# Two key projections moved in front of value products in a two-network attention kernel: the tensor engine's order changed, nothing else

## The reference, cut to what matters

```python
x = attn_layer(shift_tokens(x), Wqkv, q_scale, k_scale, Wo) + x
x = ffn_layer(shift_tokens(x), g, bln, W1, b1, W2, b2) + x

# attn_layer: 16 heads of 64, windows of 32 tokens
q, k, v = split(x @ Wqkv)              # 128 -> 3 * 1024
q = l2norm(q) * qs;  k = l2norm(k) * ksc
q = rotary(q);       k = rotary(k)     # with a scale per position
# each window of 32 queries sees its own and the previous 32 keys
sim  = where(mask, -big, q @ k.T * 8)
out  = softmax(sim) @ v
return out @ Wo
```

## Time and profile before

| what | value |
|---|---|
| median of 3 runs | 2304.53 us (2298.14 to 2307.23) |
| the profiled execution | 2299.02 us, of which the span is 2297.2 us |
| granted TensorE clock, mean | 0.987 of full speed |
| busy: PE, DVE, ACT, POOL | 93%, 77%, 75%, 58% of the span |
| first network | from about 160 to 1820 us |
| one step there | 15.3 to 18.4 us, 68.5 us for four on average |

### The profile page before, as it was taken

One profiled execution on the slowest core, in us unless ns is written; L12 is line 12 of the kernel. 1 busy time (PEld: TensorE's weight loads), 2 busy tenths in 40 slices (PEclk: granted clock), 3 DMA queues, 4 the chain that ended last, 5 costly groups with the idle time before them and its releaser, 6 DMA issues. The chain is left out here.

```text
span 2297.2 us, 88445 instructions
## 1 busy us (share of the span) xinstructions
PE 2124.9 (93%) x33790; PEld 1456.7 (63%) x33790; DVE 1760.9 (77%) x4953; ACT 1712.2 (75%) x5916; POOL 1340.2 (58%) x1270
## 2 busy tenths in 40 slices
PE   7988999999999999999999999999999886899997
PEld 5656666666666666666666666666666564666665
DVE  4988877778777878777778777877777478788873
ACT  3767788787787877787887777887788543778784
POOL 1337666666666666665676566666666124766660
PEclk8999999999999999999999999999999998999999
DMA  4001221112211222112211122111221100000001
GB/s 112 4 3 39 70 58 45 41 46 67 57 43 39 64 51 57 39 43 61 57 46 42 43 65 60 46 39 45 52 53 43 48 10 10 13 13 16 13 9 28
DMA packets 144799, 96.93 MB, mean 42 GB/s; under 512 B 61976, under 2 KB 137408, under 8 KB 144384
## 3 DMA queue, kind: packets, MB, share of 16 engines
q1 hardware_dynamic: 143232, 91.02, 15.5%
q10 hardware_dynamic: 1152, 0.26, 0.1%
HBM read 23.11 MB, written 1.05 MB: 11 GB/s over the span
## 5 line engine op out<-in xcount | busy, mean ns | idle before, releaser
L710 PE MATMUL bank<-wqkv,hs 128*128 128x512 f32 x1344 | 666.7, 614 | 19.3 <-ACT arena L1609 13.7
L1931 POOL TENSOR_TENSOR arena<-arena,rnorm 128x512 f32<-128x512 f32 x448 | 455.5, 1046 | 388.5 <-DVE rnorm L2180 387.3
L1924 POOL TENSOR_TENSOR arena<-arena 128x512 f32<-128x512 f32 x448 | 568.0, 1275 | 132.5 <-DVE arena L2129 132.2
L1578 ACT ACTIVATE arena<-bank,amx 128x64 f32<-128x64 f32 x1536 | 458.8, 336 | 8.5 <-DVE amx L2195 8.3
L2124 DVE TENSOR_TENSOR arena<-bank,rot 128x512 f32<-128x512 f32 x448 | 306.9, 685 | 82.7 <-PE bank L710 79.0
L1555 ACT ACTIVATE arena<-bank 128x512 f32<-128x512 f32 x448 | 264.4, 617 | 132.0 <-PE bank L731 130.9
L710 PEld LDWEIGHTS bank<-wqkv,hs 128*128 128x128 f32 x1344 | 228.6, 191 | 203.8 <-issue 154.9
L1578 ACT ACTIVATION_READ_ACCUMULATOR arena<-bank,amx 128x1 f32 x1536 | 352.3, 229 | 0.0
L2129 DVE TENSOR_TENSOR arena<-bank,rot 128x256 f32<-128x256 f32 x896 | 334.0, 414 | 0.0
L731 PEld LDWEIGHTS bank<-ident,arena 128*128 128x128 f32 x1792 | 212.6, 142 | 152.8 <-issue 128.3
L2136 DVE TENSOR_REDUCE ss<-arena 128x8 f32<-128x512 f32 x448 | 283.4, 670 | 32.5 <-ACT arena L1549 32.3
(11 more groups left out here) (213 smaller groups left out, 3229.8 us busy)
## 6 DMA issues: line engine op xcount, KB each, us to landing
arena<-arena SPq DMA_DIRECT2D x768, 64.0 KB
wqkv<-in_L_ffn_Wqkv_dram SPq DMA_DIRECT2D x24, 256.0 KB
hs<-z SPq DMA_DIRECT2D x128, 32.0 KB, 1.8
hs<-z SPq DMA_DIRECT2D x128, 31.8 KB, 1.9
fx<-z SPq DMA_DIRECT2D x31, 128.0 KB, 2.2
fx<-z SPq DMA_DIRECT2D x31, 127.0 KB, 2.5
wqkv<-in_L_ffn_Wqkv_dram SPq DMA_DIRECT2D x24, 128.0 KB
w<-in_L_ffn_W_dram SPq DMA_DIRECT2D x6, 341.0 KB
```

Source lines behind the costliest of these rows:

```text
L710: nc.tensor.matmul(bank[o][:], src[:], wqkv[w][:, off:off + 512], start=True, stop=True).then_inc(AT[name] if part < 2 else AT[name][i], 1)
L1578: ins = nc.scalar.activation(pb[i][0][p % 2][:, h * DH:(h + 1) * DH], bank[3 + g][:, j * DH:(j + 1) * DH], ACT.Exp, bias=amx[p % 2][:, i, ...
L1924: nc.gpsimd.tensor_tensor(t, t, rs[i][c], ALU.add).then_inc(AT["ak" if c else "aq"][i], 1)
L1931: nc.gpsimd.tensor_tensor(t, t, rnorm[p % 2][:, i, HU * c:HU * c + HU].unsqueeze(2).to_broadcast([P, HU, DH]), ALU.mult).then_inc(AT["mk" ...
```

## The change

In step s of the first network, `values_all(0, s-2)` stood at the end, behind `scores_all(0, s-1)`. It now stands in the next step, behind that step's `keys(0)`. And `keys(1, s)`, which stood behind `values_all(1, s-3)`, now stands in front of it, behind `scores_all(1, s-2)`. The waits move with the calls. The lists of DVE, ACT, POOL and SP are the same as before.

```diff
@@ step_0, the first network's step on TensorE
                         keys(0, s)
+                    if live(s - 3):
+                        at(pe, AT["ve"][1], s - 2)
+                        if live(s - 2):
+                            at(pe, AT["kte"][1], s - 1)
+                        elif live(s - 4):
+                            at(pe, AT["oe"][1], s - 3)
+                        values_all(0, s - 3)
+                    if live(s):
                         if live(s - 1):
                             at(pe, AT["sqq"], un(1, s - 1))
...
                         scores_all(1, s - 2)
+                    if live(s):
+                        at(pe, AT["sqk"], un(0, s))
+                        keys(1, s)
                     if live(s - 3):
...
                         values_all(1, s - 3)
                     if live(s):
-                        at(pe, AT["sqk"], un(0, s))
-                        keys(1, s)
                         at(pe, AT["sqq"], un(0, s))
                         queries(1, s)
...
                         scores_all(0, s - 1)
-                    if live(s - 2):
-                        at(pe, AT["ve"][1], s - 1)
-                        if live(s - 1):
-                            at(pe, AT["kte"][1], s)
-                        elif live(s - 3):
-                            at(pe, AT["oe"][1], s - 2)
-                        values_all(0, s - 2)
```

## The result

The changed kernel takes 2318.1 us (2314.1 to 2320.3, 5 runs), the one before 2304.5: the record gives a ratio of 1.0061, 95% interval 1.0040 to 1.0083. The forecast was 2320.5. The profiled execution of the changed kernel has a span of 2314.9 us, 17.7 more than before.

What follows compares the result with a forecast made beforehand. TensorE's list, busy 93% of the span, was taken to set the pace. Tile changes 32, ACT late 14 and stalls -30 gave +16 us on 2304.5, so 2320.5 us, range 2302 to 2338.

Steps and rivals of the forecast that it cites:

- The three mechanisms: TensorE's tile size changes (+32 us), ACT coming closer (+14 us), shorter idle times inside the value products (-30 us).
- Tile changes: TensorE, keys between scores and value products: 0.19 us more a unit, 36.5 us, 4.4 hidden at the GELUs: +32 us.
- ACT late: ACT starts 0.86 us later wherever it waited for value products; TensorE's waits 0.60 us per four steps: +14 us.
- the square: keys(1) waits for ACT's square of keys(0): 0.05 us late in three of four kinds of steps, 0.30 in up steps.
- the meeting at L823: Value projection and project_out need ACT's copies: 0.86 us later, the operand's load still fits under the queries; cost 0.
- The term for the turns: Broadcast step: ACT's copy of the turned keys reaches unit 1's turn late, 0.15 us for it and the turn behind.
- Stalls: Idle times of TensorE inside value products (L790) get shorter by up to 1.05 us each: -30 us, bounds 0 and -46.
- the half clock: TensorE partly at 1.2 GHz at three places, some 7 us lost; fewer stalls may avoid some: 0, 7 either way.
- no change: Rival: tile change paid, waits not, gain full: +2 us, or -1 with all stalls gone; 2305 us, chance 0.23.
- stalls only move: Rival: stalls move to queries, turns or scores: +46 us, or +31 if half saved; 2335 to 2350 us, chance 0.17.
- The faster rival: Loads of value products hide under keys, waits vanish, 30 to 46 us gained: 2276 to 2292 us, chance 0.07.
- the signs in the trace: Projection 0.95 us before value products, 0.97 behind scores; L710 waits for ACT, most in up steps; L790 issue under 20 us.

Runs made afterwards that it cites:

- unit 1's half alone: Kernel before, with only the second half of the change: keys of unit 1 between scores and value products of unit 1; 2313.0 us, ratio 1.0044.
- The run with the square first: Changed kernel, with ACT's square of unit 0's keys moved directly behind unit 0's exponentials; 2299.8 us, ratio 0.9987 against the kernel before.
- The choice of places: Kernel before, keys splitting scores and value products only in 32 places with instruction stalls (ratio 0.9904), or only in the other 160 (1.0150).
- the 32 places split: Kernel before, keys between scores and value products only in 32 of 192 places showing unhidden stalls over 0.25 us; 2276.8 us, ratio 0.9904.
- the two with the 32 places: Kernel before with keys splitting only the 32 stalling places (2276.8 us, 0.9904), and the same with ACT's square of unit 0 earlier (2286.4 us, 0.9945).

## Why the prediction was right

The three mechanisms are there, and the total is nearly the forecast one; that it is so near is in part luck, since two terms were off in opposite directions and a third was made up by the clock.

**Tile changes.** Forecast 0.19 us a unit, 36.5 us, of which the GELUs hide 4.4: 32. Measured from start to start it is 0.195: keys take 1.056 us between small tiles, where the second projection of the row took 0.861; the first projection behind the value products takes 0.96 before and after. In the mean step's half 1 it is 0.19; in the up step's half 1 it is hidden (8.49, 8.48), as forecast. It is hidden in the broadcast step's half 1 too (6.29, 6.28), by the wait for POOL, which I had not subtracted. So it is paid in six of eight half steps, 1.18 us in four steps, 28 us instead of 32.

**ACT late.** Forecast 0.60 us in four steps, 14 us. Measured, by the same division of half 2 into its pieces: 0.06 in front of the keys in mean and gate steps, 0.23 in broadcast, 0.28 in up steps, 0.05 at `project_out` in each, 0.09 at the turns of the broadcast step, 0.93 together. With 24 times that it is 22 us. Two terms were too small: the square, 0.63 instead of 0.45, most of it in the broadcast step, 0.23 where I had 0.05 (with unit 1's half alone it is 0.03 there, so it comes from unit 0's shift of ACT, which the wait for POOL doesn't take up); and the meeting at L823, where I wrote "Cost 0": ACT's copy comes while the queries run, but too late for the load to be fully hidden (0.05), 4 times in four steps. The term for the turns was too large, 0.15 against 0.09. The run with the square first took 23 us off, more than the square's 15 us of this sum: it also removed what the kernel before lost at the same place, the slower scores and, in the up step, 0.25 us in which value products waited for ACT's copy (L1586).

**Stalls.** Forecast -30 us, measured -30.2; but about 5 of these are the half clock, which the forecast put at 0 with 7 either way. The choice of places shows that these are stalls of the instruction stream, and that they are at fixed places. The Trainium skill's page Runtime: NRT & Kernel Launch (Instruction fetch mechanics) has the blocks of 256 right and calls the fetch hidden; here TensorE stood still for 47.6 us of 2297 in L790 in the kernel before.

**Sum.** 32 + 14 - 30 was +16, for 96 steps. The measured costs are 28 and 22, 50 us for 96 steps or 45.5 for the 88 steady ones, and the balance is +15.3 in the steady stretch and +17.7 over the span. The rival "no change" fell with the waits, which are there, and the rival "stalls only move" with idle time in L790 of 11.1 us, while the largest other row with "issue" (L761) grew by 2 us only. The faster rival, loads hidden under the keys, falls with 1.06 us for the keys.

What I expected of the signs in the trace came out: keys 1.06 (0.95 for entering and 0.97 for leaving, which together are 1.06), waits for L1551 most of all in up steps, L790 under 20 us.

## What to carry to other kernels

On a saturated TensorE, count changes of tile size as work: each costs about 0.1 us here though no row shows a wait, so that pieces on small tiles belong together. Against that, a dense run of tiny products used up instructions faster here than they arrived, and a long product in it hides the delay. The two pull in opposite directions; since the stalls sit at fixed places of the instruction list, split the run only there: that took 1% off, where splitting everywhere cost 0.6%. The places have to be read again after each change of the list: with the 32 places split, 1.68 us of stall appeared in a value product (at 1169.5) where before there was none. And when a consumer's cover is halved, check every later meeting of the same engine pair, weight loads too, which here lost 0.05 us each at `project_out`.

## What the runs showed of the hardware that I had not expected

A stall in the instruction stream can repeat to the hundredth of a microsecond between kernels at the same place of the list: 1.25 us at the same gate step, and at places left alone 0.89, 1.11, 0.43 and 0.38 us in the kernel before and again with the 32 places split. Others changed (1.11 became 1.38), so the place is fixed and the length is not always.

Waits and stalls trade: with the square's waits gone, stalls grew by 8 us.

The clock followed the stalls. In the steady stretch the ten profiles show 22 places with half of the clock granted, in six kernels, each of 3.4 or 6.8 us. Each begins during a stall inside value products (1.2 to 3.1 us long) or within 1.7 us of its end, as at 1062.8 around the stall of 1.82 us. Not every such stall has one, and four kernels have none: the changed one, the one with the square first, and the two with the 32 places. These have 1, 1, 5 and 3 stalls over 1.2 us there, and the others 6 to 17. So a stall costs at times more than its own length; up to 14 us a kernel here.
